# A convolution block on one core: the units of a grid of cells in another order, and VectorE's evictions spread unit by unit

## What is computed

```python
x = x + _L0_conv_ref(_gn(x), ...)   # attention in windows of 4 x 4 pixels, 16 heads of one channel
x = x + _L1_conv_ref(_gn(x), ...)   # a 3 x 3 convolution, 16 to 16 channels
x = x + _L2_conv_ref(_gn(x), ...)   # a grid of 4 x 4 cells
x = x + _L3_conv_ref(_gn(x), ...)   # a 3 x 3 convolution on inputs rounded to 8 bit by a common scale

# in _L2_conv_ref, col by col, row by row:
y = lax.conv_general_dilated(x, w, window_strides=(1, 1), padding='SAME', ...)   # 48 to 48 channels, 3 x 3
y = jax.nn.relu(y + bias[None, :, None, None])
right, up, down = jnp.split(y, 3, axis=1)
```

## Time and profile before

| | us |
|---|---|
| three runs: median (lowest, highest) | 3272.43 (3264.89, 3275.43) |
| profiled execution: time, and span from first to last instruction | 3265.59, 3263.8 |
| busy in the span: TensorE, VectorE, ScalarE | 2815.6, 2303.8, 2013.4 |
| image 0's attention, ahead of body -1 | 0 to about 293 |
| body -1; body 0 | 293.1 to 580.8; to 928.9 |
| bodies 1, 2, 3, 4 | to 1285.4; 1640.3; 1997.2; 2355.5 |
| bodies 5, 6, 7 | to 2709.3; 3032.8; 3163.5 |

### The profile page before, as it was taken

One profiled execution on the slowest core, in us unless ns is written; L12 is line 12 of the kernel. 1 busy time (PEld: TensorE's weight loads), 2 busy tenths in 40 slices (PEclk: granted clock), 3 DMA queues, 4 the chain that ended last, 5 costly groups with the idle time before them and its releaser, 6 DMA issues.

```text
span 3263.8 us, 86927 instructions
## 1 busy us (share of the span) xinstructions
PE 2815.6 (86%) x39132; PEld 1191.0 (36%) x39132; DVE 2303.8 (71%) x1977; ACT 2013.4 (62%) x2317; POOL 23.3 (1%) x67
## 2 busy tenths in 40 slices
PE   3655699989999899989998999989998989899934
PEld 2552233333333333333333333333333333333312
DVE  7977993989678995899588876889589940420224
ACT  1103976767758675766767775767676666767413
POOL 0000000000000000000000000000000000000000
PEclk9776999999999999999999999999999999999977
DMA  3003666577756766587656776586757555866566
GB/s 60 10 0 50 85 76 80 78 93 101 90 77 85 105 80 87 71 112 84 85 72 90 100 90 81 76 115 71 99 72 110 76 76 71 105 95 80 71 124 119
DMA packets 95700, 269.67 MB, mean 83 GB/s; under 512 B 79824, under 2 KB 80592, under 8 KB 83408
## 3 DMA queue, kind: packets, MB, share of 16 engines
q1 hardware_dynamic: 95312, 263.86, 60.5%
HBM read 23.01 MB, written 12.85 MB: 11 GB/s over the span
## 4 chain that ended last, share of the span: by engine, by line
PE 67%; DVE 14%; ACT 9%; issue 7%; SPq 1%; DMA 1%; POOL 0%; DVEq 0%; ACTq 0%; POOLq 0%
PE conv_banks L815 41%; PE conv_banks L829 18%; ACT pair L674 4%; ACT half L674 3%; DVE half L1003 2%; PE side_banks L742 2%; PE side_banks L776 2%; DVE pair L1003 1%; DVE score_max L1092 1%; PE stat_bank L786 1%; ACT scores L660 1%; PE conv_banks L904 1%; DVE pair L1089 1%; DVE scores L1018 1%; DVE score_max L1045 1%
## 5 line engine op out<-in xcount | busy, mean ns | idle before, releaser
L815 PE MATMUL conv_banks<-pair,w_cells 128*32 128x392 f32 x17664 | 1542.4, 498 | 46.6 <-issue 34.2
L674 ACT ACTIVATE pair<-conv_banks,b_cells 32x784 f32<-32x784 f32 x1316 | 1213.9, 922 | 597.3 <-PE conv_banks L829 531.1
L829 PE MATMUL conv_banks<-half,w_cells 64*32 64x392 f32 x18432 | 875.8, 507 | 142.2 <-ACT pair L674 64.4
L815 PEld LDWEIGHTS conv_banks<-pair,w_cells 128*32 128x32 f32 x17664 | 551.1, 109 | 981.0 <-issue 922.4
L674 ACT ACTIVATE half<-conv_banks,b_cells 32x392 f32<-32x392 f32 (+1 forms) x780 | 521.0, 668 | 204.3 <-PE conv_banks L829 128.3
L829 PEld LDWEIGHTS conv_banks<-half,w_cells 64*32 64x32 f32 x18432 | 337.4, 107 | 661.8 <-issue 609.8
L1003 DVE TENSOR_SCALAR half<-conv_banks,b_cells 32x392 f32<-32x392 f32 (+1 forms) x180 | 114.4, 636 | 333.0 <-PE conv_banks L829 174.2
L1003 DVE TENSOR_SCALAR pair<-conv_banks,b_cells 32x784 f32<-32x784 f32 x220 | 227.5, 1034 | 103.5 <-PE conv_banks L829 93.3
L1016 DVE TENSOR_TENSOR scores<-qkv 128x1792 f32<-128x1792 f32 x98 | 198.0, 2020 | 112.0 <-ACT qkv L655 111.8
L660 ACT ACTIVATE scores<-scores 128x1792 f32<-128x1792 f32 x104 | 176.8, 1700 | 93.6 <-DVE scores L1094 57.4
L1026 DVE TENSOR_REDUCE score_max<-scores 128x112 f32<-128x1792 f32 x98 | 198.0, 2020 | 9.5
...
## 6 DMA issues: line engine op xcount, KB each, us to landing
pair<-pair SPq DMA_DIRECT2D x384, 391.9 KB, 8.6
half<-half SPq DMA_DIRECT2D x352, 192.4 KB, 5.4
...
```

The lines of the kernel that those rows point to most:

```text
L674: done = nc.scalar.activation(dst, src, ACT.Relu, bias=b_ap)
L815: done = nc.tensor.matmul(conv_ps[32 * q:32 * q + 32, n + b, 0:QN], w, P[row][:, QG * s + BG * (q // 2):QG * s + BG * (q // 2 + 1), BX * ( ...
L829: done = nc.tensor.matmul(conv_ps[32 * q:32 * q + 32, n + h, 0:QN], w_all[rows, at:at + 32], T[rows, QG * u + BG * (q // 2):QG * u + BG * ...
```

## The change

The units stand in a new order, `ORDER`, in which cells are interleaved unit by unit (a star marks the units of image m); body -1 and body 7 take the units without and with a star. The sharing is by unit: `VEC_MID` names 14 units of a middle body and the attention step behind which VectorE evicts them, `VEC_LATE` 44 units of body 6 (before: 20), `VEC_LAST` 7 of body 7 (before: 16). `finish` moves from behind w6 to behind s9. Side steps have new places in all tables. In body 7 the load of the stored images waits for the last unit of rows 0 and 1 instead of a fixed count; SP comes to it at the same place, behind the send of 23R.

```diff
-BODY = [((3, 0), 1), ((2, 2), 1), ((3, 1), 1), ((2, 3), 1), ((0, 0), 0), ((3, 2), 1), ((0, 1), 0), ((3, 3), 1),
-        ((0, 2), 0), ((1, 0), 0), ((0, 3), 0), ((1, 1), 0), ((1, 2), 0), ((2, 0), 0), ((1, 3), 0), ((2, 1), 0)]
+ORDER = """
+22D0* 22U0* 30D0* 22D1* 30D1* 22U1* 00R0 22R0* 22R1* 23U0* 23U1* 31D0* 31D1* 23R0* 00D0 23R1* 00D1
+32D0* 32D1* 00R1 01D0 01D1 01R0 01U0 01U1 01R1 33R0* 33R1* 02D0 10D0 02D1 10D1 02U0 02U1 10R0 02R0
+02R1 10R1 03U0 03U1 03R0 11D0 11U0 11D1 11U1 11R0 11R1 03R1 12D0 20D0 12U0 12D1 12U1 12R0 12R1 13U0
+20D1 20R0 13U1 13R0 20R1 13R1 21U0 21D0 21D1 21U1 21R0 21R1
+"""
...
-          61: [("var1", 0, 0), ("mean0", 0, 1)], 62: [("var0", 0, 1)], 64: [("qkv", 0, 1)],
-          65: [("conv1", 0, 1)], 66: [("conv1", 1, 1)], 67: [("mean2", 0, 1), ("var2", 0, 1)]}
+PE_MID = {1: [("qkv", 1, 0)], 6: [("proj", 0, 0), ("qkv", 2, 0)], 14: [("proj", 1, 0), ("qkv", 3, 0)],
+          20: [("proj", 2, 0), ("qkv", 4, 0)], 40: [("proj", 3, 0), ("qkv", 5, 0)],
+          48: [("proj", 4, 0), ("qkv", 6, 0)], 53: [("proj", 5, 0)], 56: [("proj", 6, 0)],
+          57: [("mean1", 0, 0)], 58: [("var1", 0, 0)], 59: [("mean0", 0, 1)], 60: [("var0", 0, 1)],
+          62: [("qkv", 0, 1)], 64: [("conv1", 0, 1)], 65: [("conv1", 1, 1)], 66: [("mean2", 0, 1)],
+          67: [("var2", 0, 1)]}
...
-PE_BEFORE = {2: [("qkv", 1, 0)], 7: [("proj", 0, 0), ("qkv", 2, 0)], 12: [("proj", 1, 0), ("qkv", 3, 0)],
-             60: [("mean1", 0, 0)], 61: [("var1", 0, 0)], 64: [("conv1", 0, 1), ("conv1", 1, 1)],
+             57: [("mean1", 0, 0)], 58: [("var1", 0, 0)], 64: [("conv1", 0, 1)], 65: [("conv1", 1, 1)],
...
+ACT_MID = {0: [("qkv", 1, 0)], 1: [("exp", 1, 0)], 4: [("exp", 2, 0)], 6: [("qkv", 2, 0)], 8: [("exp", 3, 0)],
...
+           26: [("qkv", 4, 0), ("exp", 7, 0)], 40: [("exp", 8, 0), ("qkv", 5, 0)], 42: [("exp", 9, 0)],
+           46: [("exp", 10, 0)], 48: [("qkv", 6, 0)], 50: [("exp", 11, 0), ("exp", 12, 0)],
+           53: [("exp", 13, 0)], 63: [("qkv", 0, 1)], 67: [("exp", 0, 1)]}
...
-SP_MID = {35: [("x3", -1)], 48: [("xa", 2)], 63: [("conv1", 1)], 66: [("xb", 2)], 67: [("input", 1)]}
+SP_MID = {36: [("x3", -1)], 49: [("xa", 2)], 58: [("conv1", 1)], 59: [("xb", 2)], 66: [("input", 1)]}
...
-SHARED_FIRST, SHARED_MID, SHARED_LATE, SHARED_LAST = [], [(0, 0), (0, 1), (0, 2), (0, 3)], [(0, 0), (0, 1), (0, 2), (0, 3)], [(3, 0), (2, 2), (3, 1), (2, 3), (3, 2)]
+VEC_FIRST = {}
+VEC_MID = {("w", 4): "23R0 00D0",
+           ("s", 7): "00R1 01D0 01D1 01R0 01U0 01U1",
+           ("s", 8): "10D0 02D1 10D1 02U0 10R0 02R0"}
+FINISH_AT = ("s", 9)
+MOVE_AT_FIRST, MOVE_AT = ("c1", 0), ("s", 12)
...
-                    sp.wait_ge(conv_done, NS - 4)
+                    sp.wait_ge(conv_done, unit_base(m) + 1 + max(
+                        k for k, (cell, _, _) in enumerate(units_in(m)) if cell[1] < 2))
...
+            def other_work(m, at):
+
+                early = isinstance(m, int) and m < 0
+                empty(m, units((VEC_FIRST if early else VEC_MID).get(at, "")))
+                if at == FINISH_AT and not early:
+                    finish(m, m)
+                if at == (MOVE_AT_FIRST if early else MOVE_AT):
+                    move_stream(m + 1)
```

More of the change, by code:

```diff
@@ L99, in strips_of, with unit, units, starts @@
     return (u, u + 2) if has_single(col, row) else (2 * u, 2 * u + 1)
-BODY = [((3, 0), 1), ((2, 2), 1), ((3, 1), 1), ((2, 3), 1), ((0, 0), 0), ((3, 2), 1), ((0, 1), 0), ((3, 3), 1),
-        ((0, 2), 0), ((1, 0), 0), ((0, 3), 0), ((1, 1), 0), ((1, 2), 0), ((2, 0), 0), ((1, 3), 0), ((2, 1), 0)]
-EARLY_BODY = [x for x in BODY if not x[1]]
-LATE_BODY = [x for x in BODY if x[1]]
-def units_of(body):
-    return [(cell, o, u) for cell, late in body for o in cell_outs(*cell) for u in range(2)]
-UNITS_F, UNITS, UNITS_L = units_of(EARLY_BODY), units_of(BODY), units_of(LATE_BODY)
+ORDER = """
[4 more added lines that the diff above has]
+"""
+def unit(text):
+    return (int(text[0]), int(text[1])), "RUD".index(text[2]), int(text[3])
+def units(text):
+    return [unit(t) for t in text.split()]
+UNITS = units(ORDER)
+UNITS_F = [unit(t) for t in ORDER.split() if t[4:] != "*"]
+UNITS_L = [unit(t) for t in ORDER.split() if t[4:] == "*"]
 NF, NB, NL = len(UNITS_F), len(UNITS), len(UNITS_L)
 NS = NF + (B - 1) * NB + NL
-def body_of(m):
-    return (EARLY_BODY if m < 0 else LATE_BODY if m == B - 1 else BODY) if isinstance(m, int) else BODY
 def units_in(m):
-    return units_of(body_of(m))
+    return (UNITS_F if m < 0 else UNITS_L if m == B - 1 else UNITS) if isinstance(m, int) else UNITS
+def starts(m, k):
+    done = units_in(m)
+    return done[k][0] not in [cell for cell, _, _ in done[:k]]
 def unit_base(m):
@@ L147, in count_halos @@
             wrote(m, "input", INPUT)
-        for (cell, late) in body_of(m):
-            need[m, cell] = [(key, n[key]) for key in in_places(*cell)]
-            for o in cell_outs(*cell) if cell != LAST else []:
+        for k, (cell, o, u) in enumerate(units_in(m)):
+            if starts(m, k):
+                need[m, cell] = [(key, n[key]) for key in in_places(*cell)]
+            if u == 1 and cell != LAST:
                 wrote(m, (cell, o), out_place(*cell, o))
-        if m == -1:
-            n_first = dict(n)
     return need
@@ L204 @@
-SP_FIRST = {1: [("xb", 1), ("input", 0)], 30: [("xa", 2)], 44: [("conv1", 1)], 47: [("xb", 2)],
+            3: [("proj", 0, 0)], 4: [("qkv", 2, 0)], 9: [("proj", 1, 0), ("qkv", 3, 0)],
+            14: [("proj", 2, 0), ("qkv", 4, 0)], 22: [("proj", 3, 0), ("qkv", 5, 0)], 27: [("proj", 4, 0)],
+            28: [("qkv", 6, 0)], 35: [("proj", 5, 0)], 36: [("proj", 6, 0)], 38: [("mean1", 0, 0)],
+            39: [("var1", 0, 0), ("mean0", 0, 1)], 40: [("var0", 0, 1)], 42: [("qkv", 0, 1)],
+            44: [("conv1", 0, 1)], 46: [("conv1", 1, 1)], 47: [("mean2", 0, 1)], 49: [("var2", 0, 1)]}
@@ L216, in shared_in @@
+10D0 02D1 10D1 02U0 02U1 10R0 02R0 10R1 03U0 03U1 11D0 11U0 11D1 11U1 11R1 12D0 12D1 12U1 12R0 20D1
+13U1 13R0 21D0 21U1"""
+VEC_LAST = """22U0 30D1 22U1 31D0 31D1 32D0 32D1"""
+SHARED_FIRST, SHARED_MID = [[u for text in at.values() for u in units(text)] for at in (VEC_FIRST, VEC_MID)]
+SHARED_LATE, SHARED_LAST = units(VEC_LATE), units(VEC_LAST)
 def shared_in(m):
@@ L220, in n_shared @@
 def n_shared(m, end):
-    return sum(cell in shared_in(m) for cell, _, _ in units_in(m)[:end])
+    return sum(done in shared_in(m) for done in units_in(m)[:end])
 def vec_value(m, k):
-    ahead, per = n_shared(-1, NF), sum(cell in SHARED_MID for cell, _, _ in UNITS)
+    ahead, per = n_shared(-1, NF), len(SHARED_MID)
     if not isinstance(m, int):
@@ L672, in empty @@
                     return
-                for dst, src, b_ap in unit_operands(k, cell, o, u, range(2 if cell in shared_in(m) else NQ)):
+                for dst, src, b_ap in unit_operands(k, cell, o, u, range(2 if (cell, o, u) in shared_in(m) else NQ)):
                     done = nc.scalar.activation(dst, src, ACT.Relu, bias=b_ap)
@@ L1250, in _ @@
             body(B - 3)
-            body(B - 2)
-            body(B - 1)
+            late_body(B - 2)
+            late_body(B - 1)
             dve.wait_ge(main_chain, B * MAIN_CHAIN)
```

108 lines of the change are left out of this document (44 added, 64 removed).

## The result

The changed kernel takes 3328.1 us in the median (3322.9 to 3341.3) against 3270.2 before: the ratio is 1.018, with an interval of 1.015 to 1.022. It was forecast 80 us faster and came out slower, outside the range.

| us | before | forecast | after |
|---|---|---|---|
| body -1 (from 293.1) | 287.7 | 287.7 | 293.8 |
| body 0 | 348.1 | 336.4 | 347.8 |
| bodies 1 to 4, mean | 356.7 | 345.0 | 371.4 |
| body 5 | 353.8 | 338.4 | 356.5 |
| body 6 | 323.5 | 315.5 | 316.5 |

The account below looks back on a forecast made before the run. TensorE sets the pace, losing time at the top and in the middle stage of light units. -70 + 6 - 9.7 - 8 + 0 + 1.7 = -80 from 3265.6 gave 3186 us; range 3138 to 3238.

Parts of the forecast that it names:

- 7, the top of bodies 1 to 4: Top of bodies 1 to 4: nothing changed, same 9 us lost each; the gap goes with the jump back.
- third rival: Top of loop bodies: with more transfers in flight at the jump the gap doubles, 28 us: 3214 us; chance 0.08.
- Step 6: SP: x3's store waiting for finish costs nothing, slack 7; sends behind stream0's load cost body 5 6 us, once.
- fourth rival: SP's hold at the load of stream0: 21D lands 17 us late in six bodies, 3288 us; chance 0.06.
- Steps 1 to 4: Heavy stretches and light unit groups: losses of 9 us in place of 20.7, gain 11.7 in each of six bodies.
- step 3: Second light group, places 29 to 35: VectorE sets the pace, another 1.2 us; group ends at +165.1.
- Cost 0: Heavy stretches: ScalarE's eviction hides under a neighbouring unit; up to 1.6 us at 32D0 if ScalarE is behind.
- 5: VectorE's end of the body, finish now behind s9: no cost at proj6, slack 1 us.
- 8: Body 5: conv1 halves now stand before 21D1 and 21U1, send issued 13 us before; gain 9.7 us.
- 9: Body 6, without attention: loses about 16 us where it lost 23.5; gain 8 us.
- 10: First body: its conv1 wait goes, but proj0 and 00D1's eviction come later; taken as 0, between -9 and +9 us.
- 11: Tail: 23R1 no longer shared, cost 1.7 us; the wait of 29.47 us before 33R0 stays.

Follow-up runs that it names:

- the tail's run: Changed kernel with SP's stream0 load and x3 store later, TensorE's loop written out, and the seven last loads behind 32D's send: 3190.1 us, ratio 0.977.
- the extra transfers at place 54: Kernel before with transfers nobody waits for added at place 54 of each loop body: ratio 1.0005 with three of short rows, 0.9995 with six of long rows.

## Why the prediction was wrong

**The step that failed is 7, the top of bodies 1 to 4**, "same loop, same 9 us each". It measured 24.8 us: 62 us in all, more than the 58 by which the kernel got slower. Of the 141 us between the forecast and the measured span the rest is mainly the gain of the light units, some 65 us, which did not arrive (below); 9 us are body 5's first units and 6 body -1. The mechanism of the top stood in the prediction, as its third rival, at a chance of 0.08 and with half the size (7 us a body in place of 15.4). The rule of the Trainium skill cited there (page "Runtime: NRT & Kernel Launch", section Instruction fetch mechanics) is borne out: taken 12.7 us, not taken 0.08. I had read the 102 GB/s at the old top as proof that a busy DMA does little harm, and had counted bytes. The two tops show that bytes are a poor measure: 0.78 MB in the 7 us behind the jump before, in 533 packets, with the code in at once; 0.64 MB in 99 packets after, with the code late.

**Step 6, SP.** The hold was found, and its price for the halo of 21D too (forecast 6 us in body 5; measured 10.3 at 22D0, and 4.5 for a stop behind it). What was not asked is who else needs the DMA engines meanwhile. The same holds of x3's store: "no cost; slack 7" was right of the halos and missed the stops of code behind it, 26 us, which its run shows. The fourth rival had the place right, SP at the load of stream0, and the victim only in part: with the loop written out a halo wait of 9.7 us is left at each top, and the other 15 were code.

**Steps 1 to 4, the light units.** 9 us of waits were forecast and 9.6 measured in body 1, but they replace 16.9, not 20.7: some 4 us of what I called losses were no waits and stayed. The gain is 7 us a body in place of 11.7, and in the changed kernel the stops of code (7.2 us in body 1) ate all of it, so body 0 is no shorter. That the 9 was met is partly luck: VectorE is waited for 3.3 us, not some 5, and not at 10D0, while ScalarE costs 2.0 in the second group, which step 3 did not have. "Cost 0" ahead of 32D0 was 1.69 us in bodies 0 to 4 and 1.78 in body 5; the named bound was 1.6.

**Steps 5, 8, 9, 10, 11** held: TensorE has no wait at proj6; body 5's conv1 wait is gone (9.7 us at 21U0 before, none at 21D1 and 21U1 after); body 6 gained 7.0 (8 forecast); the first body lost 6.1, inside -9 to +9; body 7 grew by 1.0 (1.7), although the wait before 33R0 grew by 5.2; that the seven loads make it is shown by the tail's run, where it is 11.6. The range had the longer tops at 28 us only, and never together with a gain that fails.

**Still open:** why a held halo send delays code so much more than the other transfers. Its rows are the slowest seen here (3.2 us for 25 080 bytes, from partition to partition of SBUF). No run had other long rows in flight as far ahead of the jump as the held sends, and none with extra rows written into SBUF was tried. The Trainium skill, page "DMA: Bandwidth & Descriptors", section Back-pressure in remote DMA, says of transfers between cores that a saturated SBUF port at the destination stalls the other queues of the source's DMA engine; no run here shows whether that holds within a core. Nor was it settled why straight code stopped in the middle of bodies behind held sends, but not behind the extra transfers at place 54, beside which only one page of code a body came in.
